# An expert layer on TensorE: eight expert numbers loaded together, once in eight blocks, in place of one in each block

## What is computed

```python
def _L1_ffn_ref(hidden_states, gate_weight, e_bias, gate_proj, up_proj, down_proj):
    topk_idx, topk_w = _route(x, gate_weight, e_bias)        # 8 of 64 experts for each token
    w_full = zeros((T, 64)).at[arange(T)[:, None], topk_idx].add(topk_w)
    def step(out, ws):
        wg, wu, wd, we = ws                                  # 176x256, 176x256, 256x176
        inter = silu(x @ wg.T) * (x @ wu.T)
        return out + inter @ wd.T * we[:, None]
    ...
x = x + attention1(layernorm(x)) + ffn1(layernorm(x))
```

## Time and profile before

| | us |
|---|---|
| three runs | 1284.01, 1292.42, 1283.94 |
| median | 1284.01 |
| the profiled execution, first to last instruction | 1284.5 |
| in it: up to the first product of the expert blocks | 689.8 |
| in it: from there to the start of the last block's | 532.5 |
| in it: granted TensorE clock, mean share of full speed | 0.974 |

### The profile page before, as it was taken

One profiled execution on the slowest core, in us unless ns is written; L12 is line 12 of the kernel. 1 busy time (PEld: TensorE's weight loads), 2 busy tenths in 40 slices (PEclk: granted clock), 3 DMA queues, 4 the chain that ended last, 5 costly groups with the idle time before them and its releaser, 6 DMA issues. The chain is left out here.

```text
span 1284.5 us, 25387 instructions
## 1 busy us (share of the span) xinstructions
PE 1134.1 (88%) x7606; PEld 655.4 (51%) x7606; DVE 710.9 (55%) x2605; ACT 644.7 (50%) x1340; POOL 452.0 (35%) x525
## 2 busy tenths in 40 slices
PE   7679999999999999988976898888888888888985
PEld 3356666666666666555543444444444444444464
DVE  6486565656566666322684544554444454454557
ACT  4215554545555454643364565556555655565620
POOL 3323132222220000013103556555565655565410
PEclk9799999999999999989888999999999999999997
DMA  7401131121112011100056536525374335655257
GB/s 230 86 10 29 22 54 28 29 37 39 29 28 47 20 21 20 52 17 33 22 153 128 172 110 201 162 88 186 110 217 134 122 106 165 199 156 190 74 210 301
DMA packets 81681, 129.67 MB, mean 101 GB/s; under 512 B 32776, under 2 KB 53001, under 8 KB 81034
## 3 DMA queue, kind: packets, MB, share of 16 engines
q1 hardware_dynamic: 61576, 76.94, 21.6%
q0 software_dynamic: 15360, 47.21, 11.8%
q10 hardware_dynamic: 4616, 3.91, 1.0%
HBM read 97.57 MB, written 30.05 MB: 99 GB/s over the span
## 5 line engine op out<-in xcount | busy, mean ns | idle before, releaser
L684 DVE CUSTOM_DVE_ANT_0 a_masked<-a_ps_s,a_mask 128x512 bf16<-128x512 f32 (+3 forms) x512 | 230.0, 487 | 159.3 <-PE a_ps_s L843 155.4
L600 ACT ACTIVATE a_probs<-a_ps_e 128x512 f32<-128x512 f32 (+1 forms) x384 | 188.2, 526 | 121.7 <-PE a_ps_e L863 120.6
L1865 PE MATMUL e_ps_y<-e_w_d,e_hT 88*64 x640 | 168.6, 386 | 69.7 <-DVE e_hT L1741 62.8
L1842 PE MATMUL e_ps_gu<-e_w_gu,e_xT 128*64 x640 | 227.5, 479 | 1.0 <-ACT e_s_gu L1668 1.0
L1842 PE MATMUL e_ps_gu<-e_s_gu,e_xT 128*64 128x352 f32 x640 | 227.5, 479 | 0.0
L1635 POOL DMA_INDIRECT y<-e_y,dst x160 | 159.6, 998 | 177.0 <-DVE e_pick L1724 98.8
L189 POOL DMA_INDIRECT yn<-rows,inv x160 | 157.1, 982 | 115.7 <-DVE inv L1404 61.4
L1733 DVE TENSOR_TENSOR e_h<-e_sg,e_ps_gu 128x176 f32<-128x176 f32 x160 | 54.0, 337 | 229.3 <-ACT e_sg L1650 143.7
L1865 PE MATMUL e_ps_y<-e_s_d,e_hT 88*64 88x256 f32 x640 | 169.0, 386 | 0.0
L1865 PEld LDWEIGHTS e_ps_y<-e_w_d,e_hT 88*64 88x64 f32 x640 | 80.8, 136 | 165.8 <-issue 141.8
L843 PE MATMUL a_ps_s<-a_kT,a_qT 72*128 72x512 bf16 (+3 forms) x512 | 131.3, 300 | 12.9 <-DVE a_headmax L684 11.2
(11 more groups left out here) (243 smaller groups left out, 1899.0 us busy)
## 6 DMA issues: line engine op xcount, KB each, us to landing
e_w_gu<-e_gu SPq DMA_DIRECT2D x64, 352.0 KB
e_w_d<-e_down SPq DMA_DIRECT2D x64, 176.0 KB
a_qT<-qk_parts SPq DMA_DIRECT2D x48, 192.0 KB
e_w_gu<-y SPq DMA_DIRECT2D x12, 768.0 KB, 6.2
qk_parts<-a_stage SPq DMA_DIRECT2D x16, 256.0 KB, 2.6
e_w_gu<-y SPq DMA_DIRECT2D x4, 1024.0 KB, 7.0
qkv<-y SPq DMA_DIRECT2D x12, 256.0 KB
yn<-rows,inv POOLq DMA_INDIRECT x160
```

The costliest lines, as they stand in the source:

```text
L600: nc.scalar.activation(probs[:, i % HKV, UCOL[u]:UCOL[u + 1]], ps_e[:, (i * 3 + u) % 2, 0:w], ACT.Exp, scale=SCALE0).then_inc(exp_done, 1)
L684: ins = V.tensor_tensor_reduce(masked[:, n % 2, c:c + w], ps_s[:, n % 2, c:c + w], mask[:, T - w:T], 1.0, -3e38, ALU.add, ALU.max, headmax ...
L1842: ins = nc.tensor.matmul(ps_gu[r * SEG:(r + 1) * SEG, j % 2, 0:2 * INTER1], xT[:, j % 2, k * P + r * SEG:k * P + (r + 1) * SEG], w.rearran ...
L1865: ins = nc.tensor.matmul(ps_y[r * SEG:(r + 1) * SEG, 0:D], hT[:, j % 2, k * P + r * SEG:k * P + (r + 1) * SEG], w.rearrange("p a d -> p (a ...
```

## The change

On TensorE alone, the load of one expert number in each turn goes, and in every eighth turn eight numbers are loaded in a row. Before the loop stand the numbers of blocks 0 to 7; then, in turns 7, 15, ..., 151 (19 turns), those of the next eight blocks, at the place in the turn where the single load stood. The number of loads stays 160. Up to ten numbers are kept in registers. Nothing changes on the other engines.

```diff
+        AT_ONCE = 8
...
-            def expert_of(j):
-                return pe.value_load(seg_expert[0:1, 2 * j:2 * j + 1], min_val=0, max_val=NE - 1)
+            def experts_from(j):
+                return [pe.value_load(seg_expert[0:1, 2 * i:2 * i + 1], min_val=0, max_val=NE - 1)
+                        for i in range(j, j + AT_ONCE)]
...
-            now, before, oldest = expert_of(0), None, None
+            experts = experts_from(0)
             for j in range(NBLK + 2):
-                after = None
                 if j < NBLK:
-                    gate_up(j, now)
+                    gate_up(j, experts[j])
                 if j >= 2:
-                    down(j - 2, oldest)
-                if j + 1 < NBLK:
-                    after = expert_of(j + 1)
+                    down(j - 2, experts[j - 2])
+                if j % AT_ONCE == AT_ONCE - 1 and j + 1 < NBLK:
+                    experts += experts_from(j + 1)
                 if j + 2 < NBLK:
                     transpose_x(j + 2)
                 if 1 <= j <= NBLK:
                     transpose_h(j - 1)
-                now, before, oldest = after, now, before
```

## The result

The changed kernel takes 1376.83 us (median of 4, 1371.92 to 1379.86), the kernel before 1283.97 beside it: a ratio of 1.0715, with a 95% interval of 1.0674 to 1.0755. That is 92.9 us slower. The forecast was 1354.5, in a range of 1300 to 1380, with "slower" at 0.87. Direction and range held, the range only just (3 us from its end); the loss was forecast 22 us too small.

The account below looks back on a forecast made before the run. TensorE was taken to set the pace, with a gap of about 1.1 us in every second block. 19 x (4.3 stall + 1.0 clock - 1.7 given back) + 2 at the start = +70.4, so 1354.5 us, range 1300 to 1380.

Parts of the forecast that it names:

- The load: TensorE's sequencer: one expert-number load takes 0.65 us, and several in a row take 0.65 us each.
- The second rival: Eighth turns: loads in a row overlap, a stall of 1.8 us, no clock fall, 1286 us; chance 0.07.
- A single load's removal: Seven turns of eight: the load is covered while TensorE works on `e_ps_y`, so removing it is worth 0.
- The stall: Eighth turns, ahead of the transposes: seven more loads, 4.55 us less cover, hold TensorE up 4.3 us (4.05 to 4.45).
- The clock: TensorE after each of 19 stalls: idleness lowers the granted clock, costing 1.0 us a stall (0 to 1.6).
- Given back: Blocks after each stall: ScalarE and VectorE catch up, so fewer waits, 1.7 us back a stall (1.1 to 2.8).
- The start: Ahead of the loop, before `gate_up(0)`: seven more loads, 4.55 us, of which 2 us count (0 to 3.8).
- The sum: Whole kernel: 19 turns x 3.6 us plus 2 at the start, +70.4 us, giving 1354.9, or 1354.5 beside the median.
- The forecast's own branch: Whole kernel: stall with some recovery, 1330 to 1375 us, chance 0.52.
- The first: Expert blocks: the load delays the release of `e_sg`; 140 blocks without one give back 78 us, 1309 us; chance 0.25.
- The third: Eighth turns and after: little given back, clock paid in full, 98 us slower, 1382 us; chance 0.13.

Follow-up runs that it names:

- the one move tried: Kernel before with its one load a turn moved from behind the down products to between gate-and-up and down products: 1291.66 us against 1292.29, ratio 1.0003.
- the plain transfers: Kernel before with a block's rows brought by plain transfer in place of GpSimd's indirect gather: 1199.33 us (ratio 1.0002), once more 1201.19 (0.9997).

## Why the prediction was right, and where it fell short

**The load, 0.65 us, without overlap in a row.** Right. The steps were mostly 0.64 to 0.68 us, 0.67 in the mean. The second rival (loads overlap, 1286) is refuted.

**A single load's removal is worth nothing.** Right; with all of them gone the ratio is 0.9991.

**The stall, 4.3 us (4.05 to 4.45).** Right: 4.4 where the forecast was made, 4.2 on the other kind of chip. The transposes started 5.3 to 5.8 us behind the first load, for 5.1 to 5.4.

**The clock, 1.0 us a stall (0 to 1.6).** This step failed. It measured 2.0 to 2.3, above the upper bound. I had read 3.4 us at the lower clock from the earlier trace rows and the 0.8 us that a block lost in the earlier trace rows, a case where 2.1 of 7 us had been idle. The stall to come was twice as long, and I kept the price of the short one; the lower level then held for 6.8 us with 16 of the 19 stalls, and for 3.4 with three; on average 4.8 us of it lay behind the stall, on work. What I should have asked is how much of the lower level lies behind the stall, not how often it comes. The Trainium skill's rule (TensorE: Matmul & The Clock Gate, section HAM oscillation) that each long gap pays was right for the direction: each of the 19 stalls has a stretch at the lower level that begins in it or within 0.6 us behind it. The stage has 20 stretches in all, and that of the kernel before has 2.

**Given back, 1.7 us (1.1 to 2.8).** 32.4 / 19 = 1.7, to the tenth, for this kind of chip. The mechanism is the forecast's: one cold block and two of 2.79 us, then the waits set in again. That the number fits so well is partly luck. The forecast took all 0.56 us a block over 2.79 for waiting, 89 us in the stage, where its own view had 61.6 and the gaps add up to 68.9; in eight blocks that is 4.5 us to win for 3.4 that were there, and it left 2.8 of them for about 1.8 that remained. The two errors cancel in the difference. On the other kind it is 0. The forecast treated the waits of `e_ps_y` as a trait of the kernel, though it could not name their cause; that it came out is due to the chip on which it was tested. This is the largest thing it did not see: 31 us.

**The start, 2 us (0 to 3.8).** 4.1 by the gap ahead of `gate_up(0)`, a little above its bound; it doesn't show in the length of the one trace.

**The sum.** 19 x (4.4 + 2.0 - 1.7) + 4.1 = 93.4, against 19 x 3.6 + 2 = 70.4. Of the 23 us between them the clock is 19, stall and start the rest. The forecast's own branch was given 1330 to 1375, and 1376.83 lies just outside of that.

**The rivals.** The first, that loads make the release late, is refuted by the kernel without loads; in the changed kernel, too, "remote" waits were there in turns without a load, as the forecast had asked. The third, little given back and the clock in full (1382), has the nearer number here, 98 us for 92.9, and half of its mechanism: the clock was paid in full and more, but as much was given back as the forecast had. On the other kind of chip both halves hold, and its 98 us became 124, since nothing at all came back there. So there is luck in the range too: with the clock as measured and the recovery at its own lower bound of 1.1, the time would have been 1284 + 19 x (4.4 + 2.0 - 1.1) + 4.1 = 1389.

**What stays open** is why TensorE's semaphores come up to 2 us late in this stage on some chips. It isn't the load, nor, as far as the one move tried tells, its place. GpSimd's gather was not tried where it counts, since both runs of the plain transfers met a chip without late releases; in the kernel before, 52 of the 69 late `e_sg` start 1.6 to 2.0 us behind the start of a gather, which is a coincidence in time and no more. Nor is it known whether the recording takes part: every execution timed here was recorded too, and in the traces with late releases many updates are missing (151, 141, 149 and 111 of 161 are there for the four semaphores of TensorE in the kernel before), while on the other chips they are complete but for two in one trace.

## What to carry to other kernels

A sequencer's load is free only as long as queued work covers it. Several together don't share their cost: each that is not covered adds its 0.65 us here, while one a turn could be left in or taken out for nothing. If a batch can't be avoided, something for TensorE to do in the meantime keeps the clock up (that gave back some 36 us of 93 here). And a wait whose cause isn't known is no safe place to hide a stall in: on another chip it may not be there.

## What was not expected of the hardware

- The same program took 1200 us on some chips and 1284 to 1292 on others. The difference lies in the expert stage, 451 us (with the plain transfers) against 533. 65 of the 83 us are waits that follow from semaphores of TensorE that are released together, up to 2 us and more behind their products.
- The granted clock fell with 23 of 39 idle gaps of about 1.8 us (the shortest of them 1.65), as well as with all 19 of 4.4, and stayed up behind one of 2.05. Of the stretches at 1.2 GHz that began in the stage, 16 were 6.8 us long and 4 were 3.4 us in the changed kernel, 9 and 10 on the other kind of chip, 5 and 19 with four loads together.
- A load of one number from SBUF takes TensorE's sequencer 0.65 us, of which TENSOR_LOAD shows 0.30.
